# Ternary weights of a feed-forward layer: one scaling on VectorE, the sign at the eviction, blocks loaded in two halves

## The reference

```
s  = clip(mean(abs(w)), 1e-5, None)
wq = clip(round(w / s), -1, 1) * s          # per matrix: w1 (4096 x 1024), w2 (1024 x 4096)
```

## Time and profile before

| | before |
|---|---|
| median of 3 runs | 1059.19 us (1055.06 to 1060.83) |
| span of the profiled execution | 1054.4 us (its own time is not listed apart from the runs) |
| mean granted TensorE clock | 0.977 |
| TensorE, VectorE, ScalarE, GpSimd busy | 979.3, 737.9, 467.1, 128.0 us |
| `fq` on VectorE (L2276) | 64 instructions, 1.28 us each, from 636.0 to 759.1 |
| `fsgn` on ScalarE (L1617) | 64 instructions, 1.15 us each, from 634.7 to 756.2 |
| evictions on ScalarE (L1640, L1644) | 64 instructions, 0.60 us each, from 657.1 to 760.8 |
| transposes on TensorE (L1063) | 256, from 645.7 to 760.6 |
| loads of blocks | 64 of 512 KB, from 627.4 to 748.8 |

### The profile page before, as it was taken

One profiled execution on the slowest core, in us unless ns is written; L12 is line 12 of the kernel. 1 busy time (PEld: TensorE's weight loads), 2 busy tenths in 40 slices (PEclk: granted clock), 3 DMA queues, 4 the chain that ended last, 5 costly groups with the idle time before them and its releaser, 6 DMA issues.

```text
span 1054.4 us, 17446 instructions
## 1 busy us (share of the span) xinstructions
PE 979.3 (93%) x6781; PEld 533.9 (51%) x6781; DVE 737.9 (70%) x1038; ACT 467.1 (44%) x573; POOL 128.0 (12%) x139
## 2 busy tenths in 40 slices
PE   1799899996899999999969999899999999999998
PEld 0688655553555666665534444444444444444444
DVE  7999888877664555668679754999977555555541
ACT  5344446553355565566522113999733122222221
POOL 6300042320311111000043100011000000000000
PEclk9899899998899999999989999999999999999999
DMA  3800026665778898885446855788513554444441
GB/s 121 243 2 2 2 81 227 244 228 193 233 293 306 324 350 323 318 320 204 159 162 182 215 128 178 278 319 310 186 40 71 120 120 113 109 109 109 110 98 36
DMA packets 166145, 188.91 MB, mean 179 GB/s; under 512 B 126520, under 2 KB 126842, under 8 KB 161984
## 3 DMA queue, kind: packets, MB, share of 16 engines
q1 hardware_dynamic: 159679, 165.47, 49.1%
q0 software_dynamic: 6400, 22.55, 6.5%
HBM read 137.98 MB, written 35.33 MB: 164 GB/s over the span
## 4 chain that ended last, share of the span: by engine, by line
PE 74%; DVE 14%; issue 6%; DMA 3%; ACT 2%; POOL 0%; DVEq 0%; SPq 0%; ACTq 0%; POOLq 0%
PE ps L1095 20%; PE ps L1293 13%; PE ps L1322 12%; PE ps L1202 8%; PE ps L1218 6%; DVE fq L2276 3%; PE ps L1275 2%; PE ps L1159 2%; DMA eo_d<-eo 2%; DVE w1l L2111 2%; PE ps L982 1%; PE ps L955 1%; DVE stats L1775 1%; PE ps L973 1%; DVE o_key L1854 1%
## 5 line engine op out<-in xcount | busy, mean ns | idle before, releaser
L1293 PE MATMUL ps<-w1q,xqt 128*128 128x512 fp8e4 x640 | 139.9, 379 | 0.4 <-issue 0.4
L1656 ACT ACTIVATE hf<-ps,fs 128x512 f32<-128x512 f32 x80 | 54.9, 688 | 183.2 <-PE ps L1293 183.2
L1322 PE MATMUL ps<-w2q,hqt 128*128 128x512 fp8e4 x576 | 126.4, 379 | 0.0
L2360 DVE TENSOR_REDUCE hm<-hf 128x1 f32<-128x512 f32 x80 | 54.2, 685 | 73.8 <-ACT hf L1656 73.8
L1293 PEld LDWEIGHTS ps<-w1q,xqt 128*128 128x128 f16 x640 | 62.4, 98 | 75.8 <-issue 0.9
L1322 PEld LDWEIGHTS ps<-w2q,hqt 128*128 128x128 f16 x576 | 56.3, 98 | 66.9
L1095 PE MATMUL ps<-wt_h,xt 128*128 128x512 f16 x320 | 85.4, 379 | 0.0
L1095 PE MATMUL ps<-gwt_h,xt 128*128 128x512 f16 x320 | 84.5, 379 | 0.6 <-issue 0.6
L1202 PE MATMUL ps<-xdh,w1h 128*128 128x314 f16 x256 | 77.1, 301 | 6.2 <-ACT ht L1566 3.3
L1202 PE MATMUL ps<-xdh,w1l 128*128 128x314 f16 x256 | 76.4, 299 | 0.0
L1202 PE MATMUL ps<-xdl,w1h 128*128 128x314 f16 x256 | 76.3, 298 | 0.0
(11 more groups left out here) (320 smaller groups left out, 1949.5 us busy)
## 6 DMA issues: line engine op xcount, KB each, us to landing
wstage<-in_L_ffn_w SPq DMA_DIRECT2D x32, 1024.0 KB, 10.9
abs_in<-in_L_ffn_w SPq DMA_DIRECT2D x18, 1024.0 KB, 6.5
abs_e<-in_L_ffn_w SPq DMA_DIRECT2D x14, 1024.0 KB, 5.1
fnat_b<-in_L_ffn_w SPq DMA_DIRECT2D x28, 512.0 KB, 6.4
fnat_a<-in_L_ffn_w SPq DMA_DIRECT2D x27, 512.0 KB, 4.8
eo_d<-eo SPq DMA_DIRECT2D x16, 512.0 KB, 3.1
hq_d<-hq SPq DMA_DIRECT2D x8, 1024.0 KB, 6.3
xs_d<-xs_all SPq DMA_DIRECT2D x10, 512.0 KB, 2.9
```

Of the source, the lines that this page charges most:

```text
L1293: last = mm(ps[:, n % 4, :], xqt[:, u, k, :], w1q[:, k // 2, n * 512:(n + 1) * 512, k % 2], start=(k == 0), stop=(k == KD - 1))
L1322: last = mm(ps[:, 4 + h, :], hqt[:, u, k, :], w2q[:, k // 2, h * 512:(h + 1) * 512, k % 2], start=(k == 0), stop=(k == KF - 1))
L1656: cp(hf[:, i % 2, n * 512:(n + 1) * 512], ps[:, n % 4, :], ACT.Gelu, scale=fs[:, i % 2, 3:4]).then_inc(s_ge, 1)
L2360: last = v.tensor_reduce(hm[:, u, n:n + 1], hf[:, u, n * 512:(n + 1) * 512], AX.X, ALU.max, apply_absolute_value=True)
```

## The change

Steps 2 and 3 become one: VectorE multiplies the block by `TINY / s`, with `TINY` = 2^-9, and writes one-byte numbers. The smallest step of the one-byte format near zero is 2^-9, so the write rounds w / s to a whole number. Step 4 transposes as before. Step 5 takes the sign while it evicts, 1024 elements of one byte a partition in place of 512 of two bytes; the sign of the rounded number is -1, 0 or 1.

The pairs of rows that the matmul reads for `w1q` are now brought about by the load: the lower 64 partitions of a block get its even rows and the upper 64 its odd rows, by two transfers of 64 partitions (256 KB each). Blocks of the second matrix keep their rows and are also loaded in two halves, and the wait counts 32 a block. `fq` has four buffers, `fsgn` and its semaphore are gone, and VectorE waits for the landing of the block itself and, from the fifth block on, for the transposes four blocks back.

```diff
-        fq = sb("misc", "fq", [P, 2, D], F8)
-        fsgn = sb("misc", "fsgn", [P, 4, D], F8)
+        fq = sb("misc", "fq", [P, 4, D], F8)
...
-            f1v = f1_in.rearrange("(n p) d -> n p d", p=P)
+            f1v = f1_in.rearrange("(n z a) d -> n a z d", a=2, z=P // 2)
...
             def ternary_rows(n):
-                part = f1v[n] if n < 32 else f2v[(n - 32) // 8, n % 8]
-                sp.dma_start(fnat[n % NF], part).then_inc(s_fn[n % NF], 16)
+                for a in range(2):
+                    half = slice(64 * a, 64 * a + 64)
+                    part = f1v[n, a] if n < 32 else f2v[(n - 32) // 8, n % 8, half, :]
+                    sp.dma_start(fnat[n % NF][half], part).then_inc(s_fn[n % NF], 16)
...
             def h_high(i, u):
-                if i >= NT - 2:
-                    act.wait_ge(s_swh, 1)
-                    for n in range(2 * (i - NT + 2), 2 * (i - NT + 2) + 2):
-                        upper_sign(n)
...
-            w1p = w1q[:, :, :, :].rearrange("p c f a -> p c (f a)").bitcast(I16)
+            w1p = w1q[:, :, :, :].rearrange("p c f b -> p c (f b)")
...
             for n in range(64):
-                if 4 <= n + 3 < 64:
-                    upper_sign(n + 3)
...
-                blocks = bank16(4 + n % 4)[:, 0:D // 2].bitcast(I16)
+                blocks = bank16(4 + n % 4)[:, 0:D // 2].bitcast(F8)
                 if n < 32:
-                    part = w1p[:, :, 256 * (n // 2):256 * (n // 2) + 256].rearrange("p c (a z) -> p c a z", a=2)
-                    cp(part[:, :, :, 64 * (n % 2):64 * (n % 2) + 64], blocks.rearrange("p (c z a) -> p c a z", c=KD // 2, a=2),
-                       ACT.Copy).then_inc(s_fc, 1)
+                    part = w1p[:, :, 512 * (n // 2):512 * (n // 2) + 512].rearrange("p c (a z) -> p c a z", a=2)
+                    cp(part[:, :, :, P * (n % 2):P * (n % 2) + P], blocks.rearrange("p (c a z) -> p c a z", c=KD // 2, a=2),
+                       ACT.Sign, saturate=False).then_inc(s_fc, 1)
...
-                v.tensor_scalar(sw[:, 4:6], sw[:, 2:4], 0.5, None, ALU.mult).then_inc(s_swh, 1)
+                do(v.tensor_scalar(sw[:, 6:8], sw[:, 2:4], 1.0 / TINY, None, ALU.mult))
+                v.reciprocal(sw[:, 4:6], sw[:, 6:8]).then_inc(s_swh, 1)
                 dve.wait_ge(s_swh, 1)
-                do(v.tensor_scalar(sw[:, 6:8], sw[:, 2:4], -0.5, None, ALU.mult))
...
             def weight_piece(n):
                 m = n // 32
-                dve.wait_ge(s_fsgn, n + 1)
-                dve.wait_ge(s_ft, n + 1)
-                v.scalar_tensor_tensor(out=fq[:, n % 2, :], in0=fnat[n % NF], scalar=sw[:, 4 + m:5 + m],
-                                       in1=fsgn[:, n % 4, :], op0=ALU.is_gt, op1=ALU.min, saturate=False).then_inc(s_fq, 1)
+                dve.wait_ge(s_fn[n % NF], 32 * (n // NF) + 32)
+                if n >= 4:
+                    dve.wait_ge(s_ft, 2 + n - 3)
+                v.tensor_scalar(fq[:, n % 4, :], fnat[n % NF], sw[:, 4 + m:5 + m], None, ALU.mult,
+                                saturate=False).then_inc(s_fq, 1)
```

More of the change, by code:

```diff
@@ L67 @@
 MAGIC = 12582912.0
+TINY = 2.0 ** -9
 LN_EPS = 1e-5
@@ L446, in build_kernel @@
         s_hsfix = sem("s_hsfix")
-        s_fsgn = sem("s_fsgn")
-        s_fneg = sem("s_fneg")
         s_fq = sem("s_fq")
@@ L1060, in weight_piece @@
                 pe.wait_ge(s_fc, n + 1)
-                packed = fq[:, n % 2, :].bitcast(F16)
+                packed = fq[:, n % 4, :].bitcast(F16)
                 for k in range(KD // 2):
@@ L1610, in h_high @@
                 cp(flat[:, bass.ds(i * D, D)], h32[:, :], ACT.Copy, scale=dinv[:, 1, bass.ds(i, 1)]).then_inc(s_hsh, 1)
[L1612 to L1618, removed]
-            w1p = w1q[:, :, :, :].rearrange("p c f a -> p c (f a)").bitcast(I16)
-            w2p = w2q[:, :, :, :].rearrange("p c f a -> p c (f a)").bitcast(I16)
+            w1p = w1q[:, :, :, :].rearrange("p c f b -> p c (f b)")
+            w2p = w2q[:, :, :, :].rearrange("p c f b -> p c (f b)")
             spare = slice(LAST - 2, LAST - 2 + SEL)
@@ L1636, in _ @@
                 act.wait_ge(s_ft, 2 + n + 1)
-                blocks = bank16(4 + n % 4)[:, 0:D // 2].bitcast(I16)
+                blocks = bank16(4 + n % 4)[:, 0:D // 2].bitcast(F8)
                 if n < 32:
-                    part = w1p[:, :, 256 * (n // 2):256 * (n // 2) + 256].rearrange("p c (a z) -> p c a z", a=2)
-                    cp(part[:, :, :, 64 * (n % 2):64 * (n % 2) + 64], blocks.rearrange("p (c z a) -> p c a z", c=KD // 2, a=2),
-                       ACT.Copy).then_inc(s_fc, 1)
+                    part = w1p[:, :, 512 * (n // 2):512 * (n // 2) + 512].rearrange("p c (a z) -> p c a z", a=2)
+                    cp(part[:, :, :, P * (n % 2):P * (n % 2) + P], blocks.rearrange("p (c a z) -> p c a z", c=KD // 2, a=2),
+                       ACT.Sign, saturate=False).then_inc(s_fc, 1)
                 else:
                     b, o = (n - 32) // 8, (n - 32) % 8
-                    cp(w2p[:, 4 * b:4 * b + 4, o * P:(o + 1) * P], blocks.rearrange("p (c z) -> p c z", c=KD // 2),
-                       ACT.Copy).then_inc(s_fc, 1)
+                    cp(w2p[:, 4 * b:4 * b + 4, 2 * P * o:2 * P * (o + 1)], blocks.rearrange("p (c z) -> p c z", c=KD // 2),
+                       ACT.Sign, saturate=False).then_inc(s_fc, 1)
             def hidden_t(q, last):
```

## The result

The changed kernel takes 1077.99 us (median of 4 runs, 1072.15 to 1078.86) where the kernel before, on the same chip, takes 1057.12 (1053.03 to 1060.83): a ratio of 1.0194, 95% interval [1.0167, 1.0221], 20.9 us slower. The forecast was 1087, slower, in 1047 to 1100.

What follows compares the result with a forecast made beforehand. VectorE sets the pace before; after, block transfers: 56 blocks at 2.32 us from 656.04 plus 1.8 land at 787.8, transposes start at 788.6 instead of 760.40, so 1059.2 + 28.2 = 1087 us; range 1047 to 1100.

Steps and rivals of the forecast that it cites:

- VectorE, ScalarE: Ternary-weight stage: VectorE's new instruction near 0.75 us (8.4 a tile), ScalarE's 1024-element eviction near 1.02 us (7.2 to 8.1).
- TensorE: Ternary-weight stage: work unchanged, 8.6 + 1.54 = 10.15 us per tile, the pace if the blocks came in time.
- The transfers: Block loads in 64-partition halves through one queue: 290 ns a packet, 2.32 us a block.
- SP's issues: Block loads: SP issues 128 transfers instead of 64, at 0.33 us each, 0.66 per block, hidden.
- The sum: End of the stage: last block's transposes start at 788.6 instead of 760.40, moving the end 28.2 us to 1087.
- The clock: Ternary-weight stage: TensorE's clock falls to the lower level, some 25 us more; chance 5%, inside the slower case.
- Beside each other: Faster rival, block loads: halves run side by side, packets stay at 163 ns, about 1048 us; chance 0.26.
- Overlap half the time: Even rival, block loads: packets average 227 ns, 1.82 us a block, the loss eats the gain, 1059; chance 0.12.
- Every packet doubled: Slower rival, block loads: 2.61 us a block, transposes at 804.9, +44.5, 1104 us; within the slower 0.62.

Runs made afterwards that it cites:

- one transfer: Changed kernel with each block loaded by one 128-partition transfer, even rows of a block pair to one block, odd rows to the other: 1041.57 us, ratio 0.9862.
- the lower half alone: Kernel with one 128-partition transfer a block, but from block 9 on only partitions 0 to 63 loaded (product not that of the weights): 1042.67 us, ratio 0.9882.
- two queues: Changed kernel, but from block 9 on ScalarE's queue issues the upper halves and SP the lower: 1066.13 us, ratio 1.0094.
- Column halves: Kernel with one 128-partition transfer a block, but each block by two transfers of 128 partitions x 512 columns: 1041.44 us, ratio 0.9868.
- alternate partitions: Kernel with one 128-partition transfer a block, but each block by two transfers, each taking every second partition: 1041.97 us, ratio 0.9878.
- quarters of neighbours: Kernel with one 128-partition transfer a block, but each block by four transfers of 32 neighbouring partitions: 1078.86 us, ratio 1.0221.
- quarters of every fourth partition: Kernel with one 128-partition transfer a block, but each block by four transfers, each taking every fourth partition: 1099.96 us, ratio 1.041.

## Why the prediction was right, point by point

- **VectorE, ScalarE:** 0.75 and 1.02 taken, 0.753 and 1.023 measured. **TensorE:** 10.15 us a tile if the blocks came in time; 10.19 with one transfer.
- **The transfers** carried the verdict, and the mechanism was the right one; the term was mis-sized. The prediction took 290 ns a packet (2.32 us a block) from the gathers. Measured from the first issue to the last landing: (780.0 - 654.96 - 1.8) / 56 = 2.20 us, or 275 ns a packet. That the two lie so close is partly luck, because the 290 came from a miscount. The same two windows of the kernel before, all queues together:

```profile
DMA packets 33, 0.12 MB, mean 246 GB/s; under 512 B 3, under 2 KB 3, under 8 KB 33
...
DMA packets 26, 0.10 MB, mean 197 GB/s; under 512 B 2, under 2 KB 2, under 8 KB 26
```

Two packets in each belong to other transfers, and three and two are tiny, so the gathers have 28 and 22 packets of 4 KB, not 31 and 24: 321 and 324 ns each, at 229 and 180 GB/s instead of 254 and 197. That is the 326 ns of the lower half alone, 2.57 to 2.61 us a block, and by the prediction's own sum about 1101 us (an estimate). So the price of a lone half was taken too low, and a saving was not foreseen: halves in a row cost some 15% less than a half alone. A likely reason is that the engines are not quite in step, so that lower and upper halves overlap at the edges. That was not seen directly; the 287 GB/s of two queues speaks for it.
- **SP's issues** took 0.60 us each (median), not 0.33: 1.2 us a block, still hidden behind 2.2.
- **The sum,** 788.6 for the last transposes against 782.02: start 1.1 earlier (654.96, not 656.04), pitch 56 x 0.12 = 6.7 less, and from landing to transposes 2.0 instead of 0.85. -1.1 - 6.7 + 1.1 = -6.7, and -6.6 was measured. Of the 9 us by which 1087 was high, most of the rest is the kernel before, at 1057.12 beside the changed one and not 1059.19.
- **The clock,** given 5% and 25 us: it fell, in five of the seven tiles from 681 to 782, but cost little. The chance was too low and the price too high. The granted clock was 0.50 (1.2 GHz) from 684.75 to 688.15, behind a stretch with TensorE busy 1.01 of 3.40 us, and again at 776.91. Most of it lay in time that TensorE would have waited: from 681 to 773 the chain of what ended last holds transfers, VectorE and SP's issues, and no TensorE. On the chain only the last fall stands: 0.61 + 1.71 + 0.43 + 1.08 us where two such rounds take 2.16 at full clock (0.22 + 0.86 each), 1.7 us. The last block landed at 780.0, so at full clock its transposes could not have begun before some 780.9 (an estimate): about 1.1 us of it counts, and that is the 1.1 in the sum. With one transfer the clock stays at 1.00 in the tiles shown.
- **The rivals.** "Beside each other" gave 1048, 10.8 us of gain, from transfers that need 10.4 us a tile; with one transfer TensorE's 10.19 is the pace and the gain 14.2, so that 10.4 was too much. "Overlap half the time" (1.82 us) is what two queues reach (1.88), at 1066 rather than 1059. "Every packet doubled" is what a half costs alone, not in a row.

The best version is the one transfer a block with the new instructions: 0.9862 [0.9846, 0.9879] of before. Column halves and alternate partitions are level with it.

## What to carry to other kernels

Before a load is split by partitions, look for a row of the trace where the same number of neighbouring partitions is filled, and divide share by packets, leaving out those of a few bytes: here the busy share stayed at 1 while each packet took almost twice as long. If a layout has to come from the load, spread each transfer over all 128 partitions and let the order of rows across blocks do the work, as the one-transfer version does at no cost. A gain on the engine that sets the pace is only worth the distance to the next bound, so work out what the same edit does to that one.

## What was not expected of the hardware

- 32 neighbouring partitions load at the rate of 64 (237 GB/s both), not at half of it.
- A 4 KB packet into one half takes 166 ns while few engines write there, and 326 with all of them at work.
- The set, not the count: every second partition moves 380 GB/s where the lower and upper halves move 237.
- An issue on SP took 0.42 us (median) for quarters of neighbours and 0.59 for quarters of every fourth partition; four of the latter a block made SP the bound.
- Two queues on disjoint halves raised the rate from 237 to 287 GB/s.
